# A fused attention and mixture-of-experts kernel: in each step of the attention loop TensorE does the weighing and the next transposed score ahead of all score banks of the step

## The reference, cut to what matters

```python
q1, q2 = _rope(q1, cos, sin), _rope(q2, cos, sin)     # 16 heads, halves of width 16
k1, k2 = _rope(k1, cos, sin), _rope(k2, cos, sin)     # 4 key groups, each for 4 heads
s1 = einsum('bhtd,bhsd->bhts', q1, k1) * scale + mask # causal
s2 = einsum('bhtd,bhsd->bhts', q2, k2) * scale + mask
a1, a2 = softmax(s1), softmax(s2)
out = einsum('bhts,bhsd->bhtd', a1 - lam * a2, v)
```

## Time and profile before

| | us |
|---|---|
| median of three runs | 896.64 |
| the profiled execution | 900.73 |
| its span | 898.6 |
| PE busy in it | 760.4 |
| DVE busy | 454.1 |
| ACT busy | 341.5 |
| POOL busy | 265.9 |

### The profile page before, as it was taken

One profiled execution on the slowest core, in us unless ns is written; L12 is line 12 of the kernel. 1 busy time (PEld: TensorE's weight loads), 2 busy tenths in 40 slices (PEclk: granted clock), 3 DMA queues, 4 the chain that ended last, 5 costly groups with the idle time before them and its releaser, 6 DMA issues.

```text
span 898.6 us, 10569 instructions
## 1 busy us (share of the span) xinstructions
PE 760.4 (85%) x3572; PEld 377.6 (42%) x3573; DVE 454.1 (51%) x980; ACT 341.5 (38%) x625; POOL 265.9 (30%) x215
## 2 busy tenths in 40 slices
PE   7187899987799999868999997999986589999960
PEld 3152235333344534523454353443463346556540
DVE  2765886751667765257767546653435101111116
ACT  2315444434554433255634326556512012222213
POOL 3038610123962101087410203111211741111114
PEclk9689999999699999978999999999998879999995
DMA  3667095001037210200921014003641322111114
GB/s 120 165 107 225 19 190 84 26 18 20 24 71 141 39 49 1 36 1 24 184 42 50 0 31 147 1 3 141 236 138 35 91 15 53 41 47 41 41 48 163
DMA packets 56972, 65.32 MB, mean 73 GB/s; under 512 B 10544, under 2 KB 51008, under 8 KB 55072
## 3 DMA queue, kind: packets, MB, share of 16 engines
q1 hardware_dynamic: 52112, 58.44, 27.0%
q0 software_dynamic: 2384, 5.12, 1.6%
q10 hardware_dynamic: 2432, 1.18, 0.7%
HBM read 43.22 MB, written 21.52 MB: 72 GB/s over the span
## 4 chain that ended last, share of the span: by engine, by line
PE 67%; DVE 13%; POOL 8%; issue 5%; DMA 3%; ACT 3%; SPq 0%; ACTq 0%; DVEq 0%; POOLq 0%
PE pv_ps L956 15%; PE wide_ps L1049 10%; PE wide_ps L942 7%; PE s_ps L812 7%; DVE mneg L1411 5%; PE wide_ps L799 4%; PE pv_ps L1068 4%; PE wide_ps L926 3%; PE wide_ps L911 3%; PE s_ps L813 3%; PE misc L886 2%; POOL sorted_rows L1370 2%; PE wide_ps L931 2%; POOL work L532 2%; PE s_ps L842 2%
## 5 line engine op out<-in xcount | busy, mean ns | idle before, releaser
L1411 DVE TENSOR_REDUCE mneg<-s_ps 128x1 f32<-128x384 f32 (+3 forms) x352 | 217.1, 639 | 103.0 <-PE s_ps L813 98.5
L1196 ACT ACTIVATE w_exp<-wide_ps 128x512 f32<-128x512 f32 x320 | 180.3, 599 | 117.5 <-PE wide_ps L942 116.2
L956 PE MATMUL pv_ps<-w_exp,work 128*64 128x512 f32 x640 | 181.4, 647 | 9.4 <-POOL w_exp L1339 8.0
L812 PE MATMUL s_ps<-w_exp 96*128 96x256 bf16 (+3 forms) x512 | 138.8, 313 | 32.7 <-DMA w_exp<-q_parts 19.5
L1339 POOL TENSOR_SCALAR_AFFINE_SELECT w_exp<-w_exp 128x1024 f32<-128x1024 f32 x64 | 71.1, 1111 | 308.2 <-ACT w_exp L1196 308.2
L942 PE MATMUL wide_ps<-w_exp 98*128 98x512 bf16 x320 | 123.8, 396 | 17.2 <-ACT w_exp L1196 15.7
L813 PE MATMUL s_ps<-mask,identb 128*128 128x128 bf16 x512 | 101.8, 226 | 0.0
L942 PEld LDWEIGHTS wide_ps<-w_exp 98*128 98x128 bf16 x320 | 31.7, 103 | 159.5 <-ACT w_exp L1196 100.0
L1049 PE MATMUL wide_ps<-w_exp,tables 128*128 x184 | 89.7, 632 | 2.4 <-ACT tables L1256 0.5
L812 PEld LDWEIGHTS s_ps<-w_exp 96*128 96x128 bf16 x512 | 51.2, 100 | 69.6 <-DVE mneg L1411 37.0
L1636 DVE TENSOR_TENSOR work<-work,wide_ps 128x512 f32<-128x512 f32 x23 | 15.8, 687 | 117.2 <-ACT work L1260 117.2
(11 more groups left out here) (172 smaller groups left out, 903.3 us busy)
## 6 DMA issues: line engine op xcount, KB each, us to landing
w_exp<-q_parts SPq DMA_DIRECT2D x96, 128.0 KB, 5.4
w_exp<-w_up_in SPq DMA_DIRECT2D x8, 1024.0 KB, 8.3
work<-x_in SPq DMA_DIRECT2D x8, 512.0 KB, 5.1
w_exp<-w_down_in SPq DMA_DIRECT2D x8, 512.0 KB, 9.2
q_parts<-w_exp SPq DMA_DIRECT2D x6, 512.0 KB, 7.0
sorted_rows<-y SPq DMA_DIRECT2D x1, 2944.0 KB, 13.8
tables<-sorted_rows SPq DMA_DIRECT2D x23, 128.0 KB, 2.0
w_exp<-k_parts SPq DMA_DIRECT2D x18, 128.0 KB, 3.9
```

The source lines that it names most:

```text
L812: nc.tensor.matmul(o, q_stack[0:KROWS, qt, hs, :], keys[0:KROWS, gs, 0:qt + 1, :], start=True, stop=False)
L956: last = nc.tensor.matmul(pv_ps[s * 64:(s + 1) * 64, :], vo[:, kt, g, :], probs[:, n % NP, s, :], start=(kt == 0), stop=(kt == qt))
L1196: nc.scalar.activation(probs[:, n % NP, s], st_bank(v), ACT.Exp, scale=float(DH) ** -0.5).then_inc(st_done, 1)
L1411: nc.vector.tensor_reduce(out=mneg[:, qt, rows[0]:rows[-1] + 1], in_=s_ps[:, (v - 1) % 2, 0:len(rows) * w].rearrange("p (r k) -> p r k", r ...
```

## The change

PE's part of a step is written in another order. Before, the banks of a step were cut in two parts, the first of (number + 1) // 2 banks, and the weighing and the first transposed score of step n + 2 stood between the parts. Now those two come directly behind the second transposed score of step n + 1, and all banks of the step follow, then the tasks.

```diff
                     if n + 1 < NSTEP:
                         scores(b, n + 1, 1)
 
-                    now = banks_at(b, n)
-                    for part in (0, 1):
-                        if part == 1 and n > 0:
-                            weigh(b, n - 1)
-                        if part == 1 and n + 2 < NSTEP:
-                            scores(b, n + 2, 0)
-                        for qt, i, back in (now[:(len(now) + 1) // 2], now[(len(now) + 1) // 2:])[part]:
-                            if i == 0:
-                                await_stacks(b - back, qt)
-                            score_bank(b - back, qt, i)
+                    if n > 0:
+                        weigh(b, n - 1)
+                    if n + 2 < NSTEP:
+                        scores(b, n + 2, 0)
+                    for qt, i, back in banks_at(b, n):
+                        if i == 0:
+                            await_stacks(b - back, qt)
+                        score_bank(b - back, qt, i)
                     for name, arg, back in tasks_at(n, prep_next, post):
                         task(name, arg, b - back)
```

## The result

The changed kernel took **929.23 us**, the median of four runs (924.15 to 930.73), against 898.87 us for the kernel before on the same chip (four runs, 894.23 to 901.59). The ratio is 1.0352, 95% interval 1.0313 to 1.0392: 3.5% slower, 28 to 35 us. The forecast was +21.5 us and 906 to 928. The sign and the main mechanism (the third and fourth bank of a step wait for DVE) were right. The size was a third too small, and the time lies just outside the range.

The account below looks back on a forecast made before the run. PE was taken to bound the kernel, so only its waits count: -22.0 old, +42.6 new, +0.9 for `mt` gave +21.5 us. That put the median at 918 us, range 906 to 928.

Parts of the forecast that it names:

- old waits: PE's existing waits for DVE's reductions ahead of score banks, in batches 0, 1 and 2, would go: -22.0 us.
- unit prices: PE time lost per third bank in a row: 0.45 us for `qt` 0, 0.61 `qt` 1, 0.59 `qt` 2, 0.65 `qt` 3.
- step 28: In batches 1 and 2 DVE comes late to its first bank; PE would lose 2.2 us in one wait, not 1.9 in two.
- `mt` of step 39: It waits for the reduction of the last of two banks, which DVE reaches 0.3 us later: 0.9 us in all.
- Rival 2: The short PE waits let the clock fall in the three later stages: 14 us lost, 933 us; chance 6%.
- At other tasks DVE is no later: Outside `mt` of step 39 tasks cost nothing, since a third bank filled late is also reduced at once.
- Steps with two banks* ... nothing: 16 steps in each of batches 1 to 3, 7 in each later half: two PSUM banks hold them, so no cost.
- New waits: PE waits for DVE at third and fourth banks in batch 0 and in later halves of batches 0 to 2: 42.6 us.
- step 8: In batch 0, where DVE's slow splitting of the maxima made PE stand 2.15 us, the wait would stay about 2.2 us.
- The factor 0.53: Turns the profile's double-counted idle time before L812 into real loss, from one wait: 0.37 us lost for 0.70 idle.
- The bounds: Low: new waits cost only their idle part, +10.4 us, 907. High: 69 two-bank steps lose 0.1 us each, +28.4, 925.
- The rule weighed in the prediction: Short idle times while cycling through PSUM banks make the clock fall and rise repeatedly; the kernel would then match the second rival.

Follow-up runs that it names:

- the last experiment: The changed order in every step but 17 and 18 of each batch, which keep the order before; 933.37 us, ratio 1.0296 against the kernel before.

## Why the prediction was wrong in size

**Right.** PE sets the time, the old waits went and new ones came. The unit prices built up from the timeline held (the measured one first, the forecast one behind it): 0.59 and 0.59 us for the third bank of `qt` 2, 0.61 and 0.61 for `qt` 1, 0.67 to 0.74 and 0.65 for `qt` 3, 0.48 to 0.55 and 0.45 for `qt` 0 where nothing collides, 2.13 and 2.2 in step 28, 1.43 and 1.5 for `mt` of step 39. Rival 2, a fallen clock as the main loss (14 us), is out: the clock is 1.00 from 291 to 383 us with fourteen waits. But the clock was not without a part, as told below. `mt` and step 28 of batch 2:

```profile
556.52 0.22 PE L882 MATMUL misc<-identb,msplit 128*128 128x128 bf16 x1 [1.43 <-DVE msplit L1416]
```
```profile
505.26 0.34 PE L812 MATMUL s_ps<-w_exp 96*128 96x384 bf16 x1 [1.97 <-DVE mneg L1409]
...
505.55 3.14 PE L926 MATMUL wide_ps<-x2T,w_sh 128*128 128x512 f32 x4
```

**The step that failed** is "At other tasks DVE is no later", and with it "*Steps with two banks* ... nothing". I asked only whether a reduction comes late because its bank is filled late. I did not ask when POOL's instructions fall, though the change moves them against DVE's. The row for it was there: the CAST of 1.15 us in the earlier trace rows, which I took as slow and fixed. Before it ran beside an instruction of POOL's of 2.13 us from 103.55 on and ended 0.03 us behind it, and in the changed kernel the same instruction takes 0.26 us. What this and the rest made of the sum:

- *New waits,* forecast 42.6, measured 46.9 us. The collision in step 18 adds 0.55 us to step 19 in batches 1 and 2 and 0.22 in batch 0 (shown by the last experiment). In batch 0 two more places have the same picture (waits of 1.83 and 1.06 us at banks that were priced 0.59, behind DVE instructions of 2.25 and 1.24 us in place of 0.35), which no run isolated. Against that, step 8 lost 1.09 us and not 2.2: there DVE's CAST took 0.26 us this time. The fourth banks lost 0.23, not 0.30.
- *Old waits,* forecast 22.0, measured 20.4. The factor 0.53, from one wait, was a little high for the others: 1.6 us.
- *Batch 3,* forecast 0, measured +3.6 in this execution and +3.3 by the comparison of batch 3 alone. About 1 us of it is step 18's collision, shown by two experiments. Another 1.0 us is step 3, which takes 5.50 or 5.51 us in all four traces that have its collision. The last 1.3 us lie in steps 4 to 6, and there the granted clock is lower. The stretch from the weighing of step 4 to that of step 7, in the kernel before, in the changed one and in the one with batch 3 alone changed (columns as in the earlier trace rows, the granted clock is the third number from the end):

```profile
554.80:568.30 13.50, 11.16 (x52) 5.20 (x50) 7.48 (x17) 6.56 (x14) 2.32 (x3) 0.87 0.00 1
580.40:595.20 14.80, 13.73 (x51) 5.93 (x50) 7.32 (x17) 6.39 (x13) 2.31 (x3) 0.65 0.00 1
553.80:565.70 11.90, 11.18 (x53) 5.17 (x52) 7.35 (x17) 6.38 (x13) 2.32 (x3) 0.86 0.01 2
```

  The same matmuls keep PE busy for 13.73 us at a mean of 0.65 and for 11.16 at 0.87. Whether the changed order brings this fall about is open: in the third trace, with the same collision in step 3, it does not come, these steps are 1.6 us shorter than before, and the start of its batch 3 takes 55.0 us, no longer than before. So the net cost of step 3's collision differs from execution to execution.
- *The clock,* forecast 0, in batch 2's later half. The row of 505.55 shows four matmuls in 3.14 us behind the wait of 1.97 us; the same four in batch 1, behind an equal wait, take 1.94. The windows around the two are:

```profile
505.00:509.00 4.00, 3.74 (x8) 1.20 (x8) 1.34 (x4) 0.21 (x1) 0.00 (x0) 0.64 0.42 137
330.00:334.00 4.00, 3.52 (x13) 1.26 (x14) 2.14 (x5) 1.20 (x3) 0.00 (x0) 1.00 0.42 135
```

So batch 2's later half lost 9.9 us where batch 1's lost 8.3: at 505 us the clock was partly at 1.2 GHz, at 330 us at 2.4 throughout, behind equal waits. It is not a single case. The three experiments that make the bank of step 28 wait likewise (the third bank behind the score, steps of three or four alone, steps 17 and 18 old) have one such fall each, at the same place in batch 1 or in batch 2, and that later half is 1.6 us longer than the other. The kernel before has none there in either trace. In the start of batch 0 the clock's mean is 0.93 in place of 0.95 before. With the changed order in the steps of three or four banks alone it is 0.97, and that start is 2.7 us longer, not 5.3; what of the difference is the clock's is open.

With the loop at +31.9 and a forecast of +21.6, the 10.3 us are: new waits 4.3, old waits 1.6, batch 3 3.6 (1.3 of it in steps with a lower clock), clock in batch 2 1.6, less 1.2 in the start of batch 2; the remaining 0.4 is spread. Some of the near fit is luck: 1.1 us less at step 8 and 1.2 in the start of batch 2 offset other misses.

**The bounds** were drawn around the price of a bank, the term that turned out sure. The upper one (0.1 us in each of 69 steps with two banks, +28.4) was near the size for the wrong reason: most steps of two banks lose nothing, and a few with a collision lose about 1 us.

**The rules of the pages.** The collision is described by the Trainium skill, page "SBUF — State Buffer", section "Who interferes with whom": DVE and GpSimd share a pair of ports, a DVE instruction with two SBUF inputs contends with a GpSimd instruction that reads SBUF, one in a two-port mode contends with GpSimd as well, and whoever issues first has the pair for its whole instruction. The traces agree: DVE's 1.03 and 1.06 us end 0.14 and 0.04 us behind POOL's 1.09. The same section says that a reduction never contends. The traces agree there too: in the changed kernel 36 reductions of 384 columns ran wholly beside a POOL instruction and 83 beside none, and both took 0.55 to 0.56 us.

The rule weighed in the prediction, the Trainium skill's "TensorE: Matmul & The Clock Gate", section "A second HAM failure mode: psum-queue depth-cycling", did not set the time: the granted clock was 0.934 over the span against 0.933, with more than twice the time lost ahead of the banks (46.9 us for 20.4). In batch 1's later half it stayed at 1.00 through all fourteen waits, and in batch 2's a fall stands behind the one wait of 2 us.

## What to carry to other kernels

With two PSUM banks between PE and a reader, what counts is PE's other work between a bank and the next but one: keep at least the reader's time (0.87 us for 384 columns here) there, and spread banks one to a gap, which gave 2 to 6 us here. When work is moved on one engine, follow also the engines that it feeds: list the small DVE instructions that run near POOL's large ones, and ask which of the two now comes first. A price built from one step of the timeline was good to a tenth of a us here; most of the error sat in the terms that were set to nothing.

## What the runs showed of the hardware

- A DVE instruction of 0.18 or 0.35 us that starts 0.06 to 0.20 us behind POOL's mask takes 1.03 to 1.06 us. If DVE comes 0.12 us ahead it keeps its 0.35 us, and POOL's takes 1.18 for 1.09. The loop of the kernel before has 12 such SCALAR_TENSOR_TENSOR or CAST instructions that take at least 0.25 us too long beside work of POOL, the changed one 19.
- From PE's last matmul of a bank to DVE's start are 0.25 us, from the reduction's end to PE's next fill 0.10. With the reduction cut to an eighth, a third bank in a row still loses 0.23 us.
- After a PE wait of 1.97 us the granted clock was 0.64 over 4 us in one batch (partly 1.2 GHz) and 1.00 in another (2.4 GHz), with the same work before. In batch 1 that wait, one of 0.87 and twelve of 0.4 to 0.5 us (as idle), in 92 us, left the clock at 1.00.
